# Wait counts of a graph network kernel from 16-bit unsigned tables

## What is computed

```python
x = _layernorm(x + _L0_gnn_ref(x, src, dst, w1, b1, w2, b2))        # degree-normed sum of neighbours, two matmuls
x = _layernorm(x + _L1_gnn_ref(x, fc, attn, src, dst, edge_type_8)) # attention, 8 relations, 1 head
x = _layernorm(x + _L2_gnn_ref(x, src, dst, eps, W1, b1, W2, b2))   # sum of neighbours, two matmuls
x = _layernorm(x + _L3_gnn_ref(x, edge_attr_64, src, dst, ...))     # attention, 4 heads, edge features
...
msg = hn[src] * attn[:, :, None]
out = jax.ops.segment_sum(msg, dst, num_segments=n)
```

## Time and profile before

| | us |
|---|---|
| median of 3 runs | 11083.2 |
| lowest and highest run | 11058.91, 11108.54 |
| span of the profiled execution | 11064.0 |
| PE busy | 3739.3 (34%) |
| DVE busy | 3269.5 (30%) |
| ACT busy | 228.8 (2%) |
| POOL busy | 6323.3 (57%) |

### The profile page before, as it was taken

The page is one execution under the profiler, slowest core; times in us unless marked ns, Lnnn a source line. Parts: engine busy times, 40 slices in busy tenths (PEclk is TensorE's granted clock), DMA queues, the critical chain, the costliest instruction groups (busy, mean ns, idle before and its releaser), DMA issues. The chain is left out here.

```text
span 11064.0 us, 65181 instructions
## 1 busy us (share of the span) xinstructions
PE 3739.3 (34%) x16686; PEld 3432.3 (31%) x16691; DVE 3269.5 (30%) x3857; ACT 228.8 (2%) x792; POOL 6323.3 (57%) x6584
## 2 busy tenths in 40 slices
PE   7333333335222233333323332333412222233333
PEld 6333333334222232332323332333412212223223
DVE  7100101004211121221224454544522222332323
ACT  0000000002000000000000000000000000000000
POOL 6666666665554455655366666666454444555552
PEclk5555555555555555555555555555555555555555
DMA  3311111112111111111111111111121111111110
GB/s 56 61 23 23 23 23 23 23 23 87 23 19 18 18 20 22 22 20 22 27 42 47 48 48 47 49 49 45 34 44 20 20 19 22 22 25 25 24 25 18
DMA packets 334682, 345.48 MB, mean 31 GB/s; under 512 B 183228, under 2 KB 212360, under 8 KB 327850
## 3 DMA queue, kind: packets, MB, share of 16 engines
q0 software_dynamic: 209952, 220.30, 11.6%
q1 hardware_dynamic: 124676, 124.51, 3.9%
HBM read 304.50 MB, written 40.68 MB: 31 GB/s over the span
## 5 line engine op out<-in xcount | busy, mean ns | idle before, releaser
L1175 POOL DMA_INDIRECT rows_a<-table,idx_c_a x1612 | 1536.9, 953 | 1405.7 <-ACT idx_c_a L1142 924.1
L1175 POOL DMA_INDIRECT rows<-table,idx_c_a x1612 | 1544.7, 958 | 1188.5 <-ACT idx_c_a L1142 706.7
L701 PE MATMUL acc_a<-msg_a,hot_a 128*128 x6640 | 1614.6, 422 | 1414.3 <-issue 1224.9
L938 POOL DMA_INDIRECT rows_l<-table,idx_c_l x1612 | 1524.9, 946 | 900.4 <-issue 493.1
L701 PEld LDWEIGHTS acc_a<-msg_a,hot_a 128*128 128x128 f32 x6640 | 1486.8, 327 | 1527.3 <-issue 1520.2
L938 POOL DMA_INDIRECT rows<-table,idx_c_l x1548 | 1463.4, 945 | 834.5 <-issue 468.4
L967 DVE TENSOR_TENSOR hot_l<-side_l,neg_tl 128x2048 f32<-128x2048 f32 x208 | 472.0, 2283 | 3140.0 <-remote 2864.3
L701 PE MATMUL acc_l<-rows_l,hot_l 128*128 x3320 | 779.5, 388 | 1578.5 <-issue 1466.5
L701 PEld LDWEIGHTS acc_l<-rows_l,hot_l 128*128 128x128 f32 x3320 | 770.1, 322 | 1588.6 <-issue 1588.0
L701 PE MATMUL acc_l<-rows,hot_l 128*128 x3320 | 783.2, 390 | 1404.9 <-issue 1313.7
L701 PEld LDWEIGHTS acc_l<-rows,hot_l 128*128 128x128 f32 x3320 | 768.4, 322 | 1420.4 <-issue 1419.8
(11 more groups left out here) (298 smaller groups left out, 2541.8 us busy)
## 6 DMA issues: line engine op xcount, KB each, us to landing
feat<-edge_attr SPq DMA_DIRECT2D x50, 1031.2 KB
rows<-table,idx_c_a POOLq DMA_INDIRECT x1612
rows_l<-table,idx_c_l POOLq DMA_INDIRECT x1612
rows_a<-table,idx_c_a POOLq DMA_INDIRECT x1612
rows<-table,idx_c_l POOLq DMA_INDIRECT x1548
table<-stage SPq DMA_DIRECT2D x49, 260.0 KB
spread<-zero SPq DMA_DIRECT2D x12, 832.0 KB
hot_a<-spread SPq DMA_DIRECT2D x2, 3328.0 KB
```

What stands on the lines that cost most here:

```text
L701: return nc.tensor.matmul(acc[:, bass.ds(at, row.shape[-1])], hot, row, start=False, stop=True, skip_group_check=True)
L938: pool.indirect_dma_start(rows[:, half * BODY + s * CH + k, 0:D], None, table, bass.IndirectOffsetOnAxis(idx_c[:, s, k:k + 1], 0))\
L1175: pool.indirect_dma_start(rows[:, u, k, 0:row], None, table, bass.IndirectOffsetOnAxis(idx_c[:, u, k:k + 1], 0)).then_inc(gathered[u], 16)
```

## The change

Four kinds of counts that engines wait for are kept in 16-bit unsigned tables in place of 32-bit ones: `lands`, `frees`, `start_s` (with their tiles and DRAM copies), and the needed messages, which were row 3 of `offs` and are now a table of their own, `needs`, on partition 0. `offs` keeps its three rows of places, in 32 bits. SyncE writes and reads `needs` with two transfers of its own, and its waits count four transfers in place of three. The third load ahead of every 8 visits reads `needs`. The semaphores, the counts and the places of the waits are as before.

```diff
@@ tables
-        offs = sb("offs", [4, V], I32)
-        lands = sb("lands", [1, VCHUNKS, SLOTS], I32)
-        frees = sb("frees", [1, VCHUNKS], I32)
+        offs = sb("offs", [3, V], I32)
+        lands = sb("lands", [1, VCHUNKS, SLOTS], U16)
+        frees = sb("frees", [1, VCHUNKS], U16)
+        needs = sb("needs", [1, V], U16)
...
-        start_i = sb("start_i", [P, G], I32)
+        start_i = sb("start_i", [P, G], U16)
         at_s = sb("at_s", [1, GS], I32)
-        start_s = sb("start_s", [1, GS], I32)
+        start_s = sb("start_s", [1, GS], U16)
...
-            off_i = tsb("off_i", [P, 4, G], I32)
-            land_i = tsb("land_i", [P, G, SLOTS], I32)
+            off_i = tsb("off_i", [P, 3, G], I32)
+            land_i = tsb("land_i", [P, G, SLOTS], U16)
...
-            free_i = tsb("free_i", [P, G], I32)
+            free_i = tsb("free_i", [P, G], U16)
+            need_i = tsb("need_i", [P, G], U16)
@@ SyncE, setup
-                    sp.dma_start(offs_d.rearrange("(n g q) -> q n g", n=4, q=P), off_i[:], allow_slow_non_contiguous=True).then_inc(off_out, 16)
+                    sp.dma_start(offs_d.rearrange("(n g q) -> q n g", n=3, q=P), off_i[:], allow_slow_non_contiguous=True).then_inc(off_out, 16)
...
-                    sp.wait_ge(off_out, 48)
-                    sp.dma_start(offs[:], offs_d.rearrange("(n v) -> n v", n=4)).then_inc(off_in, 16)
+                    sp.dma_start(needs_d.rearrange("(g q) -> q g", q=P), need_i[:], allow_slow_non_contiguous=True).then_inc(off_out, 16)
+                    sp.wait_ge(off_out, 64)
+                    sp.dma_start(needs[:], needs_d.unsqueeze(0)).then_inc(off_in, 16)
+                    sp.dma_start(offs[:], offs_d.rearrange("(n v) -> n v", n=3)).then_inc(off_in, 16)
...
-                    sp.wait_ge(off_in, 48)
+                    sp.wait_ge(off_in, 64)
@@ DVE, setup
-                    nc.vector.tensor_scalar(off_i[:, 3], q[:], 1.0, None, ALU.add).then_inc(off_ready, 1)
+                    nc.vector.tensor_scalar(need_i[:], q[:], 1.0, None, ALU.add).then_inc(off_ready, 1)
@@ TensorE, attention layers
-                                need = table(3, g, lo, size, 1, PIECES_OF * (GS - 1) + -(-LAST // PIECE))
+                                need = nc.values_load_multi_w_load_instructions(
+                                    needs[0:1, bass.ds(g * S + lo, size)], engines=PE_ONLY, min_val=1, max_val=PIECES_OF * (GS - 1) + -(-LAST // PIECE),
+                                    skip_runtime_bounds_check_because=BOUNDED)[1]
```

More of the change, by code:

```diff
@@ L28 @@
 I32 = mybir.dt.int32
+U16 = mybir.dt.uint16
 ALU = mybir.AluOpType
@@ L224, in build @@
         edges_d = dram("edges_d", (T, P), I32)
-        offs_d = dram("offs_d", (4 * V,), I32)
+        offs_d = dram("offs_d", (3 * V,), I32)
         lo_d = dram("lo_d", (EARLY_ROWS * (T - 1),), BF16)
-        lands_d = dram("lands_d", (V, SLOTS), I32)
-        frees_d = dram("frees_d", (V,), I32)
+        lands_d = dram("lands_d", (V, SLOTS), U16)
+        frees_d = dram("frees_d", (V,), U16)
+        needs_d = dram("needs_d", (V,), U16)
         et_d = dram("et_d", (VP,))
@@ L239, in build @@
         at_d = dram("at_d", (V,), I32)
-        start_d = dram("start_d", (V,), I32)
+        start_d = dram("start_d", (V,), U16)
         def rows_of(flat):
```

## The result

The changed kernel took 11307.3 us in the median of four runs (11297.84 to 11316.21), the kernel before 11085.75 us in four (the three of the table ahead and one more): ratio 1.0207, 95% interval 1.0178 to 1.0237. The forecast was 11083 us with a range of 11015 to 11150, so the time lies outside the range and on the side that had been given a chance of 0.10. The profiled execution spans 11296.1 us, 232 us more than the one before.

The account below looks back on a forecast made before the run. It took a serial chain of about 30 us plus POOL's 60 us of gathers to make each attention group's period. All terms were put at 0, leaving the median at 11083 us, with a range of 11015 to 11150.

Parts of the forecast that it names:

- The bound by the chain: Attention layers: one serial chain of about 30 us plus POOL's 60 us of gathers make a group's period.
- The price of the needs load: TensorE's 416 loads of eight needed messages: priced by value, staying at 590 ns, change 0; chance 0.72.
- handled twice: Upper bound for a needs load, 1106 ns: 0.516 us more, 34 us over 66 loads or 119 over 230.
- The matmuls cover the loads: Attention layers: TensorE's sequencer runs ahead, so matmuls hide the sets of loads after a group's first.
- if that cover were gone: All sets ahead of DVE's rescaling would be on the chain, some 230 loads: 59 us less or 119 more.
- 66 exposed sets: First set before each group's visits, 33 groups in two layers, is exposed: 17 us less by byte, 34 more upwards.
- Rival B: A 16-bit load costs more, behind the probabilities: 34 us more, 11117, or 119 more, 11202; chance 0.08.
- Lands, frees and start at 0: The 200 lands, 186 frees and 66 start loads change the time by 0; lands at best 11 us less.
- the rival by bytes: Loads priced by bytes: needs 333 ns, lands 0.055 us less; 28 us less, or 70 with all exposed; chance 0.12.
- Setup at 0: SyncE's added setup transfers, about 6 us and at most 31, are covered by its wait for DVE's scaled features.
- Rival C: Groups fall otherwise into the stretches where loads take 700 ns: say 60 us either way, 11023 or 11143; chance 0.08.

Follow-up runs that it names:

- ladder: A kernel computing no layer, only loading 1 to 16 values from 32-bit and 16-bit rows into registers; eight 16-bit values took 1920 ns, eight 32-bit ones 587.
- half_hoist16: Changed kernel with every other attention-layer gather left out and each group's first three loads moved into earlier TensorE gaps: 7924.65 us, 226 us below the same without the move.
- hoist32: Changed kernel with needs in 32 bits, a max operation at each wait, and each group's first three loads moved earlier: 11186.0 us, ratio 1.0170, slower kind.
- before_max: Kernel before with one register operation more, max(value, 0), at each wait on a loaded value: 11235.62 us, ratio 1.0212, slower kind.
- after_again: The changed kernel as it is, run again on a second chip of the slower kind: 11226.28 us, ratio 1.0202.
- needs16: Changed kernel with only needs in 16 bits and its own table; lands, frees and start back in 32 bits: 11248.56 us, ratio 1.0228, slower kind.
- hoist16: Changed kernel, still 16 bits, with each group's first three loads moved into earlier TensorE gaps: 8757.52 us, ratio 1.0033, quicker kind.
- needs32: Changed kernel with needs in 32 bits again and a max operation at each of its waits: 8749.31 us, ratio 1.0023, quicker kind.

## Why the prediction was wrong

**The bound by the chain: right on its chip, and only there.** One serial chain plus POOL's 60 us was the right reading of the earlier trace rows: in groups 2 to 6 some 1.2 of the 1.33 us at the first visit come out at the next index copy, group by group. On the quicker kind the chain runs beside the gathers, POOL does not wait for it, and the kernel before needs 8730 us.

**The price of the needs load: the step that failed.** The prediction says "I take the price by value, since one register is written for each value in both cases", 590 ns, and puts the upper bound at 1106 ns, "the nearest costlier row". It was 1924 ns. Value, byte and short values "handled twice" were all tried on a row of four points, and the rows spoke against the first two: from 1 to 4 values the load grows by 55 ns, from 4 to 8 by 257, from 8 to 16 by twice 258. A price by value or by byte would make three more values 192 ns dearer. The durations go in steps of four 32-bit values, and then the question to ask was whether 16-bit values go in fours as well. They do not: 0.23 us for each one, 1920 ns for eight (ladder). The upper bound was no bound, as it took a 32-bit row for the costliest form; with the step of 0.26 us from 4 to 8 values taken once for every value, an estimate, it would have been 8 x 0.26 = 2.1 us. That a short value is "cut out of a word and widened" no run shows.

**"The matmuls cover the loads".** Right for 3 x 0.59 = 1.8 us ahead of eight visits of 3.56. Wrong for 0.59 + 0.59 + 1.92 = 3.1 us together with what else the sequencer does for eight visits: gaps of 1.03 to 1.27 us. The prediction had this as what happens "if that cover were gone", with 230 sets, and had named 0.24 us as the point from which it decides; the load went up by 1.33.

**66 exposed sets: right in place, an upper end in size.** 66 x 1.33 = 88 us of the 190, if every group pays its first set in full. half_hoist16 shows that without cover; on the slower kind groups 2 to 11 pay it, and hoist32 against before_max shows 0.3 us a group left of it in the later part of a1.

**Rival B was what happened, with its price term mis-sized**: 0.516 us instead of 1.33. Its own two sums with the measured load give 66 x 1.33 = 88 us with the first sets alone and 230 x 1.33 = 306 with all sets ahead of the rescaling. With 1.2 us for an inner set (the gaps) the second is 88 + 164 x 1.2 = 285; 190 were paid. The stepwise rise of the group differences shows inner sets being paid one by one up to group 12. That groups 19 to 28 of a1 pay only 0.9 to 1.7 us again is read off the same differences; why the inner sets are cheap there, whether because they lie in the slow stretch, was not isolated.

**Lands, frees and start at 0: right.** Lands rose by 0.66 us, against the "0.055 us less" of the rival by bytes, yet the gather layers moved by -1.2 and +1.9 us. **Setup at 0: right for the change, wrong for the trace.** SyncE still waits for DVE's scaled features behind its added transfers (156.2 us in place of 127.3), so they were covered, and the 41 us belong to the setup's two ranges of end times, the later one seen in before_max without the change. The forecast had that wait fall to some 121 us; the hole in DVE's work made it longer instead. So of the 232 us between the profiles 190 stand in the layers that the change makes longer. The medians differ by 221.55 us.

**Rival C (stretches fall otherwise) is not idle.** a3's groups 12 to 17 differ by 10.1, 7.8, 2.1, 5.4, 8.4 and 7.8 us, and two of these are more than the 6 x 1.33 = 8.0 us by which all needs loads of a group grew. The six sum to 42 us, those of a1 to 16, and in after_again and needs16 a3's sum to 26 and 25. before_max shows how a little more work in TensorE's queue grows in the slow stretch. It is part of how the loads are paid on the slower kind, and its share in the 190 us stays open.

No version here beats the kernel before on either kind of chip. hoist16 on the slower kind was the candidate, and it stays unmeasured. Also not run: needs as a 32-bit table of its own without the added operations, on the slower kind, which would price the width there directly.

## What to carry to other kernels

A register load is priced neither by its bytes nor by its values alone. Keep such tables in 32 bits, start rows at multiples of four values and load multiples of four: 333 ns for four (the lands, which begin at multiples of four, and the ladder) and 587 for eight, where four from an offset of one took 1000 and eight from an offset of two 1933. The 16-bit type left loads of one and two values nearly as they were (301 and 533 ns, then 287 and 520) and made those of four, eight and sixteen from the start of the row 3.0 to 3.4 times as long (333, 587 and 1101 ns, then 987, 1920 and 3787). From a few durations first ask whether they lie on a line or on steps, and bound an unseen form by the highest step taken once for every value. Before a wait or load is costed at nothing, divide the cover: a set of loads that is hidden at 1.8 us per 3.56 us of matmuls is not hidden at 3.1. And take the ratio only from runs on the same chip: what is hidden on one chip is paid on another.

## What the runs showed of the hardware that was not expected

- A load of four 32-bit values from the start of the row takes 333 ns, less than one of two (533 ns) and a third of one of four from an offset of one (1000 ns); eight 16-bit values take 1920 ns, eight 32-bit ones with a stride of two 1921 (all ladder).
- The same program takes 8730 or 11086 us, by the chip or its condition, with gathers of nearly the same price in the attention layers (951 to 960 ns in before and after, 957 to 967 in hoist16 and needs32, and 0.30 us between them in all). In the traces of the slower kind TensorE's matmuls come some 2.8 us apart, here and there 3.5, in the later part of POOL's gathers, in both kernels; two rows of the changed one:

```profile
8784.66 0.27 PE L707 MATMUL acc_a<-msg_a,hot_a 128*128 x1 [2.52 <-issue]
8787.47 0.27 PE L707 MATMUL acc_a<-msg_a,hot_a 128*128 x1 [2.54 <-issue]
```

  The granted TensorE clock is 0.50 to 0.51 in the profiled executions of this kernel on both kinds. The cause is open.
- On the slower kind one register operation more at each wait on a loaded value, nothing else, cost 2.1% of the time (before_max), by the traces mostly in the later groups of the attention layers.
